# A transformer block on one core: a new order of work in the prologue, in every batch's middle and in the expert tail

## The reference

```python
mod = (silu(c) @ wmod)            # six vectors of 256 per batch: sa, ca, ga, sb, cb, gb
ga, gb = sign(g) * max(|g|, 0.25)
h = layernorm(x) * (1 + ca) + sa
x = x + ga * attention(h)         # 16 heads, low-rank q (192) and kv (64), rope on 64, causal
h = layernorm(x) * (1 + cb) + sb
x = x + gb * ffn(h)

def ffn(x):                                     # x: 4096 tokens
    scores = softmax(x @ gate_w.T)              # 16 experts
    topk_w, topk_i = top_k(scores, 4)           # weights normed to sum 1
    # every expert takes its first 128 tokens (CAP), in token order; the others are dropped
    for e in range(16):
        xg = x[buf[e]]                                     # 128 tokens
        eout = (silu(xg @ w_gate[e]) * (xg @ w_up[e])) @ w_down[e] * wbuf[e]   # inner 176
        y[buf[e]] += eout
    return y + (silu(x @ sw_gate) * (x @ sw_up)) @ sw_down # shared part, inner 352
```

## Time and profile before

| | us |
|---|---|
| median of 3 runs | 1293.26 |
| profiled execution, its own time | 1287.12 |
| its span, first to last instruction | 1285.3 |
| busy PE / DVE / ACT / POOL | 1193.3 / 848.6 / 667.5 / 279.6 |

### The profile page before, as it was taken

How to read it: one execution, slowest core, us unless ns; L and a number is a source line. 1 busy time by engine, 2 the same in 40 slices (tenths; PEclk the granted TensorE clock), 3 DMA queues, 4 the chain that set the end, 5 groups by cost and what they waited for, 6 DMA issues and landing times.

```text
span 1285.3 us, 25913 instructions
## 1 busy us (share of the span) xinstructions
PE 1193.3 (93%) x7556; PEld 954.7 (74%) x7556; DVE 848.6 (66%) x2579; ACT 667.5 (52%) x1922; POOL 279.6 (22%) x332
## 2 busy tenths in 40 slices
PE   6699999999999999999999999999999999995874
PEld 4488877887688768887788768886888768882542
DVE  3367757776687668775777668766877677756221
ACT  1367634675367626764477526762577346741220
POOL 1000022211322132212221122113212132202553
PEclk8799999999999999999999999999999999998985
DMA  9510002000010001000100001000100000003762
GB/s 305 139 45 0 0 1 65 3 0 0 16 49 0 0 16 49 0 0 0 45 20 0 0 16 49 0 0 16 49 0 0 0 30 20 0 1 100 213 150 37
DMA packets 48317, 46.17 MB, mean 36 GB/s; under 512 B 10048, under 2 KB 44960, under 8 KB 48296
## 3 DMA queue, kind: packets, MB, share of 16 engines
q1 hardware_dynamic: 29096, 30.90, 8.3%
q0 software_dynamic: 7168, 6.37, 2.8%
q10 hardware_dynamic: 12032, 8.65, 2.3%
HBM read 35.04 MB, written 15.11 MB: 39 GB/s over the span
## 4 chain that ended last, share of the span: by engine, by line
PE 78%; DVE 9%; DMA 5%; issue 3%; ACT 2%; POOL 2%; POOLq 0%; DVEq 0%; SPq 0%; ACTq 0%
PE PS L675 11%; PE PS L696 10%; PE PS L654 7%; PE PS L655 6%; PE PS L656 6%; PE PS L797 6%; DMA out<-x_res,toku 5%; PE PS L640 5%; PE PS L805 3%; PE PS L827 3%; PE PS L788 2%; PE PS L627 2%; PE PS L630 2%; PE PS L631 2%; PE PS L628 2%
## 5 line engine op out<-in xcount | busy, mean ns | idle before, releaser
L973 ACT ACTIVATE probs<-probs,nmax 128x512 f32<-128x512 f32 (+3 forms) x512 | 283.1, 554 | 127.0 <-DVE nmax L1229 123.1
L1229 DVE CUSTOM_DVE_ANT_0 probs<-PS,cmask 128x512 f32<-128x512 f32 (+3 forms) x512 | 229.3, 488 | 101.0 <-PE PS L656 97.9
L538 POOL DMA_INDIRECT tab_dram<-entry,slot x112 | 110.5, 986 | 389.9 <-PE PS L696 368.6
L654 PE MATMUL PS<-kTh,qTh 128*128 128x512 f32 (+3 forms) x512 | 176.9, 345 | 0.6 <-DVE qTl L1260 0.6
L982 ACT ACTIVATE pT<-PS 128x384 f32<-128x384 f32 (+3 forms) x320 | 126.8, 462 | 77.9 <-PE PS L675 77.9
L675 PE MATMUL PS<-ident,probs 128*128 128x128 f32 x1280 | 165.7, 276 | 0.0
L656 PE MATMUL PS<-kTh,qTl 128*128 128x512 f32 (+3 forms) x512 | 165.4, 323 | 0.0
L655 PE MATMUL PS<-kTl,qTh 128*128 128x512 f32 (+3 forms) x512 | 165.4, 323 | 0.0
L696 PE MATMUL PS<-pT,kmat 128*64 128x512 f32 (+3 forms) x1024 | 152.0, 439 | 0.3 <-issue 0.3
L675 PEld LDWEIGHTS PS<-ident,probs 128*128 128x128 f32 x1280 | 142.4, 141 | 10.3 <-issue 7.4
L696 PEld LDWEIGHTS PS<-pT,kmat 128*64 128x64 f32 x1024 | 68.0, 136 | 76.0 <-issue 62.1
(11 more groups left out here) (237 smaller groups left out, 2112.8 us busy)
## 6 DMA issues: line engine op xcount, KB each, us to landing
x_in<-in_x SPq DMA_DIRECT2D x8, 512.0 KB, 5.9
modb<-mod_dram SPq DMA_DIRECT2D x8, 512.0 KB, 5.4
h_dram<-mod_dram SPq DMA_DIRECT2D x1, 4096.0 KB
h_dram<-h SPq DMA_DIRECT2D x8, 512.0 KB, 3.0
out<-base SPq DMA_DIRECT2D x8, 512.0 KB
pT<-in_wo SPq DMA_DIRECT2D x1, 2048.0 KB, 11.7
tab_dram<-entry,slot POOLq DMA_INDIRECT x112
oT<-in_wqnT SPq DMA_DIRECT2D x1, 1536.0 KB, 10.2
```

What stands on the lines that cost most here:

```text
L538: pool.indirect_dma_start(tab_dram[:, :], bass.IndirectOffsetOnAxis(ap=slot[:, j:j + 1], axis=0), entry[:, j, :], None, bounds_check=NE * ...
L654: pe.matmul(PS[:, bank, 0:n], qTh[:, h, rows_q], kTh[:, 0:n], start=True, stop=False)
L973: act.activation(probs[:, UO[u]:UO[u] + UW[u]], probs[:, UO[u]:UO[u] + UW[u]], ACT.Exp, scale=-1.0, bias=nmax[:, u:u + 1], accum_out=psums ...
L1229: dve.tensor_tensor_reduce(out=probs[:, UO[u]:UO[u] + UW[u]], in0=PS[:, SBANK[u], 0:UW[u]], in1=cmask[:, S - UW[u]:S], scale=-1.0, scalar= ...
```

## The change

Three parts. **Prologue:** the input and the key/value weights are loaded earlier; PE turns the first batch's input before absorbing; the modulation is turned in the middle of the first absorbing pass; the second pass stands behind the keys and values; the output projection is absorbed behind the first query projection; DVE makes the residual gates after the modulation of the first batch. **Middle:** the product with the last third of the shared weights and the router is split by tokens, the first three tiles (384 columns) before the last tile is turned and its 128 columns after; ACT copies the first queries before the last tile; POOL's scaling of the normed rows also waits for rope. **Last batch and tail:** seats are found by token and choice (16 pairs of tile and choice, 128 seats each); the inner dimension 176 is cut 88 + 88 instead of 128 + 48; POOL adds two experts at a time. For that, PE turns the token numbers (`turn_tokens`), DVE marks which tokens of the odd expert the even one has too (`same_tokens`), PE carries the shared tokens' rows over (`merge`), DVE adds them to the even expert's rows (`merge_out`), and the odd expert's addition leaves them out (`destu`).

```diff
@@ sync
+            sp.dma_start(x_in[:], rows(xr, 0)).then_inc(x_landed, 16)
             for dst, src in ((wqn_st[:, :, 0:QL], wqnT), (wqn_st[:, :, QL:], wqnT[:, :, P:QL])):
                 sp.dma_start(dst, src.rearrange("h p n -> p h n")).then_inc(wq_in, 16)
             sp.dma_start(wk_st, wkT).then_inc(wq_in, 16)
-            sp.dma_start(x_in[:], rows(xr, 0)).then_inc(x_landed, 16)
+            sp.dma_start(wkva_sb[:], wkva.rearrange("(c p) n -> p c n", p=P)).then_inc(wk_in, 16)
...
@@ gpsimd, post
                 pool.wait_ge(h2T_ps, 3 * (b + 1))
+                if n is not None:
+                    wait_alone(pool, rope_ready, n * NPAIR + 1)
                 pool.tensor_tensor(h2[:], h2[:], spread(2), ALU.mult).then_inc(h2_scaled, 1)
...
@@ gpsimd, tail
-            for e in range(NE):
-                pool.wait_ge(ey_ready, e + 1)
-                if e:
-                    pool.wait_ge(added, 16 * e)
...
-                if e + ROWS_AHEAD < NE:
-                    gather_rows(e + ROWS_AHEAD)
+            for k in range(NE // 2):
+                pool.wait_ge(merged_ready, k + 1)
+                if k:
+                    pool.wait_ge(added, 32 * k)
+                scatter_add(2 * k + 1, destu[:, k:k + 1])
+                scatter_add(2 * k, toku[:, 2 * k:2 * k + 1])
+                for e in (2 * k + ROWS_AHEAD, 2 * k + 1 + ROWS_AHEAD):
+                    if e < NE:
+                        gather_rows(e)
@@ tensor, last batch and experts
-                    for e in range(NE):
-                        col = 6 * (t * NE + e)
-                        mm = pe.matmul(PS[:, 2, col:col + 6], onehot[t % 2][:, e, :],
...
+                    for k in range(t * TOPK, (t + 1) * TOPK):
+                        mm = pe.matmul(PS[:, 2, 0:6 * NE], onehot[:, k, :],
+                                       spread_parts[:, k, :, :].rearrange("p e c -> p (e c)"),
+                                       start=k == 0, stop=k == NT * TOPK - 1)
...
+            def merge(k):
+                pe.wait_ge(ey_ready, 2 * k + 2)
+                if k:
+                    pe.wait_ge(merged_ready, k)
+                pe.matmul(PS[:, 5, 0:H], same[:, k, :], ey[(2 * k + 1) % NT],
+                          start=True, stop=True).then_inc(merge_ps, 1)
+
+            turn_tokens()
             turn_rows(0)
             for e in range(NE):
                 gate_up(e)
...
                 if e >= 2:
                     down(e - 2)
+                if e >= 4 and e % 2 == 0:
+                    merge(e // 2 - 2)
             turn_inner(NE - 1)
             down(NE - 2)
+            merge(NE // 2 - 2)
             down(NE - 1)
+            merge(NE // 2 - 1)
@@ tensor, middle
                 if post:
+                    pe.wait_ge(x1_ready, 3 * b + 3)
+                    ffn_router(b, 0, (3, 4))
                     pe.wait_ge(n2_ready, 2 * b + 2)
                     turn_h2_last()
-                    ffn(b, 2, (3, 4))
+                    ffn_router(b, 1, (3, 4)).then_inc(gu_ps, 1)
@@ vector
+                dve.tensor_tensor(spread_parts, oh[:].rearrange("p t k e -> p (t k) e").unsqueeze(3).to_broadcast(
+                                      [P, NT * TOPK, NE, 6]),
+                                  parts[:].rearrange("p k c m -> p k (c m)").unsqueeze(2).to_broadcast(
+                                      [P, NT * TOPK, NE, 6]), ALU.mult).then_inc(parts_ready, 1)
...
                 for t in range(NT):
-                    if t >= 2:
-                        dve.wait_ge(placed_ps, t - 1)
-                    dve.tensor_tensor(onehot[t % 2], seat[:].unsqueeze(1).to_broadcast([P, NE, P]),
+                    k = slice(t * TOPK, (t + 1) * TOPK)
+                    dve.tensor_tensor(onehot[:, k, :], seat[:].unsqueeze(1).to_broadcast([P, TOPK, P]),
...
+            def same_tokens():
+                dve.wait_ge(token_ps, 1)
+                odd = tab[:].rearrange("p (k o) c -> p k o c", o=2)[:, :, 1, 0]
+                ch.step(dve.tensor_tensor(same, PS[:, 6:8, :].rearrange("p a (k s) -> p (a k) s", s=P),
+                                          odd.unsqueeze(2).to_broadcast([P, NE // 2, P]), ALU.is_equal))
+                ch.step(dve.tensor_reduce(matched[:], same, AX.X, ALU.max))
...
                 if e >= NT:
-                    dve.wait_ge(added, 16 * (e - NT + 1))
+                    dve.wait_ge(added, 32 * (e // 2 - 1))
...
+            def merge_out(k):
+                dve.wait_ge(merge_ps, k + 1)
+                dve.tensor_tensor(ey[2 * k % NT], PS[:, 5, 0:H], ey[2 * k % NT],
+                                  ALU.add).then_inc(merged_ready, 1)
```

## The result

The changed kernel takes 1275.96 us (median of 4 runs, 1274.53 to 1280.13) beside 1293.22 for the kernel before on the same chip: a ratio of 0.987, 95% interval 0.985 to 0.990, or 17 us less. The prediction was 1291.7 with a range of 1277 to 1304, so the direction was right, the size was not, and the time fell out of the range on the side of the gain. The profiled execution took 1276.56 us (span 1274.7), 10.6 less than the profiled execution of before (1287.12), which is not one of the timed runs of before.

The account below looks back on a forecast made before the run. The prediction took PE to bound the batches, and chains through several engines the prologue and tail. Its sum −10.4 (prologue) −15.4 (middles) +24.2 (last batch and tail) = −1.6 gave 1291.7 us for the median run, range 1277 to 1304.

Parts of the forecast that it names:

- the loop's turn: Tail: gathers wait behind a pair's additions, a closed loop run five times; 13.5 to 17.7 us, taken as 16.1.
- the way to the first pair: Tail: from the start of the expert rounds to the first pair's addition, 17.6 us where it was 9.9.
- Prologue, −10.4 predicted: Prologue: keys and values start 11.0 us earlier, 0.6 lost to the output absorption; gain 10.4, bounds 6.7 and 13.
- the 7.09 + 1.0: Prologue: one absorbing pass at most 7.09 us, turning the modulation between its halves about 1.0; pass ends at 25.6.
- if L618 takes twice as long at the lower level: Prologue: lower bound, the output absorption taking twice its 3.67 us; gain then 6.7.
- 13 if the first step then runs at the upper: Prologue: upper bound, the first step running at PE's upper clock level; gain then 13 us.
- Middles, −2.2 each predicted: Seven middles: divided product and undisturbed rope turn the queries 2.2 us earlier each, 15.4 in all; bounds 9 to 19.
- that rival (1307.1): Middles: POOL's moved work blocks DVE later, or something else holds L640, so they give nothing; 1307.1 us, chance 0.09.
- Last batch, −7.0 predicted: Last batch: cheaper seats (4.1 us) and the split router product (2.9) start the expert rounds at 1190.0, not 1197.0.
- Tail, +31.2 predicted: Tail: later first pair and five slow turns of pairs waiting for gathers; end at 1309.5, 24.2 later.
- the pairs pay as they read: Tail rival: gathers land before they are needed, a pair costs 7.5 us; whole 1249, chance 0.06.
- no change: Whole kernel: a change under 0.2% (2.6 us) can't be told from none; chance of same 0.18.

Follow-up runs that it names:

- e4: The kernel before once more, no edit, for a second profile; 1287.0 us profiled.
- e1: The changed kernel with the gathers ahead of the wait for each pair, not behind its two additions; 1239.5 us, ratio 0.962 to before.
- e6: The changed kernel with the router's product undivided and ACT's copies in the old order, POOL's wait for rope kept; 1283.2 us, ratio 0.997 to 1.000.
- e7: The changed kernel without POOL's wait for rope, the product still divided; 1271.0 us, ratio 0.988 to 0.992.
- e8: The changed kernel with the last batch's seats found by expert as before; 1274.0 us, ratio 0.990 to 0.994.
- e12: The changed kernel again, no edit; 1271.4 us, ratio to before 0.988 to 0.991.
- e3: The kernel before with the new prologue alone; 1272.2 us, ratio 0.985 to 0.988.

## Why the prediction was wrong

The mechanisms were right in the main, and two terms of the sum failed in size: the prologue's by 4.2 and the tail's by 4.4. Both made the forecast too slow. In the prologue the step that failed is the stretch behind the turned queries, which the sum kept at its length of before, a term put at nothing. In the tail it is the length of the loop's turn and of the way to the first pair.

**Prologue, −10.4 predicted, −14.6 in the trace.** The prediction's own point is the turned queries: it had them 10.4 earlier, and they came 11.25 earlier (49.23 for 60.48). Three misses nearly cancel there. Keys and values started 1.8 earlier than said, because the absorbing pass took 2.00 + 0.66 + 2.00 and not the 7.09 + 1.0 of rows at the lower clock; ahead of that pass PE had stood for 1.93 us before, and between 18 and 22 us the clock fell from 1.00 to 0.50; now it stands for 1.31, and the clock stayed up. Their products took 4.54 and not 6.19, which brings what follows them another 1.7 forward. But from the first query projection to the turned queries it took 8.8 (40.46 to 49.23), where the sum had 6.1: after waits of 3.70 and 2.12 this stretch ran at the lower clock. The case "if L618 takes twice as long at the lower level" was named for it, and L631 took 4.30.

The larger part, 3.35, lies behind the turned queries. From them to the first middle it took 104.4 before and 101.06 after, and the sum had no term for it. Before, PE idled 2.89 ahead of the turned queries and then worked for some 15 us partly at the lower clock; now the output absorption fills that wait, and the clock stays up. PE's busy time and granted clock, before and then after:

```profile
60.00:70.00 10.00, 8.96 (x44) 0.66 0.63 161
70.00:80.00 10.00, 8.14 (x53) 0.83 0.16 49
```

```profile
60.00:70.00 10.00, 9.15 (x71) 1.00 0.62 157
70.00:80.00 10.00, 10.00 (x76) 1.00 0.21 50
```

The prediction named this as its bound, "13 if the first step then runs at the upper", and did not count it. It is the steady part of the gain. Thirteen traces of this prologue without fillers have this stretch at 101.0 to 101.1 (before: 104.4 and, in e4, 103.4), while their turned queries come anywhere from 46.5 to 51.5 by where the clock fell. So their first middles lie at 147.5 to 152.5, mean 150.5, which is 12.4 to 17.4 earlier than before. A duration at the lower clock was taken from a row and kept for a place ahead of which PE waits less.

**Middles, −2.2 each predicted, −2.1 in the first two traces, −2.5 on the chip of e1 to e4.** On the other chips no trace of before exists; there the changed kernel has 137.0 to 137.6. Right in size and in mechanism, with one correction: the prediction named the division and POOL's wait together as what removes rope's stretch; e6 and e7 show that either does, and that the wait is idle beside the division. No later instruction of DVE was stretched; that rival (1307.1) is out.

**Last batch, −7.0 predicted, −8.0 in the trace.** The seats were put at 4.1 and are worth 3.6 to 4.7 (e8).

**Tail, +31.2 predicted, +26.8 in the trace.** The mechanism held in each part: PE waits 7.3 for the gathers, five times; e1 removes the loop and gives back 33 to 35. The size is 1.1 too large for the first pair (16.5 and not 17.6) and 2.9 for the five turns (15.96, 14.83, 15.97, 14.79, 15.89 against 16.1 each): every second turn had less low clock than the 5 us I took for each. Behind the rows that land at 1199.42 PE works 4.0 at the lower clock, behind those at 1244.98 6.2. The rest (7.5, 6.5, 7.1) was predicted within 0.4 each. The rival "the pairs pay as they read" had the right mechanism too: with the gathers in time a pair costs the 7.5 that it named, from the fourth pair on and until the order of `merge_out` and `weigh` is changed.

These four make −10.6 where the prediction had −1.6. The remaining 6.7 us of the measured 17.3 is the difference between the first profiled execution of before and its timed runs, which the prediction added to both kernels alike; after shows no such difference, and the cause stays open. The repetition on another chip gives 13.8 with an interval of 12.0 to 15.8. So 1291.7 was off by 9 in its own terms. With e12's ratio the time would have been 1279, inside the range, so that the edge at 1277 was missed by 1 is in part chance of the chip. That the direction came out right says little too: the forecast −1.6 was less than the 2.6 that it called no change.

## What to carry to other kernels

Before an instruction is made to serve two items at once, look at what stands behind it in its queue: the pair was worth 10 us over single additions, and the tail lost 26.8 because the gathers of the next items waited behind it. A transfer that feeds the pipeline belongs ahead of a wait for the pipeline's end. A duration read at one clock level is a bound and not a value for a place with another wait ahead of it: take both levels into the range.

## What the runs showed of the hardware

The granted clock differs between executions of one program: after and e12 are the same kernel, and its mean from 40 to 50 us was 0.69 in one and 0.95 in the other. It differs after short waits too: it fell in a wait of 1.2 us that began at 22.6 us in e3, and not in the same wait of e1. Over thirteen traces of this prologue the first middle moved by up to 5 us. Holding it up with extra products in three waits moved the drop to a later stretch. In the tail, where PE idled 7.3 us in each turn, fillers kept a mean of 0.97 in place of 0.71 and gave 2 us a turn. The landing of an accumulating DMA took 5.2, 4.9 and 4.6 us in the first three pairs of e1, where the core's DMAs moved 247 to 151 GB/s, and 3.9 in the next two at 90. The same kernel before took 1284.9 to 1293.2 us on the chips of this study, and the distance between middles of the changed kernel was 137.0 on two of them and 137.3 to 137.8 on the others.
